# Order of VectorE's work in each step: the lows of a step's weights before the weight sums of the next step

## What is computed

```
f     = relu(einsum('bld,ldf->bf', x, W_enc) + b_enc)   # x: 512 x 2 x 1024, W_enc: 2 x 1024 x 4096
x_hat = einsum('bf,lfd->bld', f, W_dec) + b_dec         # W_dec: 2 x 4096 x 1024
```

## Time and profile before

| | |
|---|---|
| runs | 671.85, 672.27, 672.31 us |
| the profiled execution | 672.02 us |
| its span (first to last instruction) | 670.2 us |
| TensorE busy | 645.5 us, 96% |
| VectorE busy | 577.0 us, 86% |
| ScalarE busy | 339.9 us, 51% |
| mean granted TensorE clock | 0.993 |

### The profile page before, as it was taken

The page is one execution under the profiler, slowest core; times in us unless marked ns, Lnnn a source line. Parts: engine busy times, 40 slices in busy tenths (PEclk is TensorE's granted clock), DMA queues, the critical chain, the costliest instruction groups (busy, mean ns, idle before and its releaser), DMA issues.

```text
span 670.2 us, 8024 instructions
## 1 busy us (share of the span) xinstructions
PE 645.5 (96%) x2892; PEld 525.2 (78%) x2892; DVE 577.0 (86%) x755; ACT 339.9 (51%) x425; POOL 18.3 (3%) x26
## 2 busy tenths in 40 slices
PE   6799999999999999999999999999998999999996
PEld 3577888888887888888888888787876878887785
DVE  6999989889999856659897599999999999997844
ACT  4555335445465445455666657444555454464442
POOL 0000000000000000000000000001102011011000
PEclk9799999999999999999999999999999999999999
DMA  8956676655565565555645475569968889689624
GB/s 299 340 183 195 196 231 187 190 189 179 161 187 184 183 205 172 181 161 173 189 145 189 156 235 191 178 221 225 304 196 230 251 231 270 209 197 308 211 108 156
DMA packets 69446, 137.38 MB, mean 205 GB/s; under 512 B 5152, under 2 KB 5152, under 8 KB 69408
## 3 DMA queue, kind: packets, MB, share of 16 engines
q1 hardware_dynamic: 66528, 126.40, 58.0%
q0 software_dynamic: 2880, 10.49, 8.5%
HBM read 122.18 MB, written 4.19 MB: 189 GB/s over the span
## 4 chain that ended last, share of the span: by engine, by line
PE 69%; DVE 21%; DMA 4%; issue 4%; ACT 1%; SPq 1%; DVEq 0%; ACTq 0%
PE sums L568 22%; PE sums L570 22%; PE sums L569 22%; DVE w_split L368 8%; DVE w_raw L368 5%; PE sums L580 3%; DVE forms L368 3%; DMA w_raw<-w_dec 3%; DVE s_sum L368 2%; DVE place L368 2%; DMA w_raw<-w_enc 1%; ACT w_split L265 0%; ACT place L305 0%; ACT place L318 0%; ACT forms L283 0%
## 5 line engine op out<-in xcount | busy, mean ns | idle before, releaser
L265 ACT CAST w_split<-w_raw 128x1024 fp32r<-128x1024 f32 (+1 forms) x255 | 240.0, 945 | 288.2 <-PE sums L570 225.2
L568 PE MATMUL sums<-w_split,forms 128*128 128x512 f32 x896 | 355.3, 396 | 17.1 <-DVE w_split L368 12.9
L570 PE MATMUL sums<-w_split,forms 128*128 128x512 f32 x896 | 350.1, 391 | 0.0
L569 PE MATMUL sums<-w_split,forms 128*128 128x512 f32 x896 | 349.8, 390 | 0.0
L368 DVE TENSOR_TENSOR w_split<-w_raw,w_split 128x1024 fp32r<-128x1024 f32 (+1 forms) x257 | 269.1, 1082 | 59.6 <-ACT w_split L265 59.0
L568 PEld LDWEIGHTS sums<-w_split,forms 128*128 128x128 f32 x896 | 168.7, 188 | 59.9 <-issue 18.1
L570 PEld LDWEIGHTS sums<-w_split,forms 128*128 128x128 f32 x896 | 168.7, 188 | 36.2
L569 PEld LDWEIGHTS sums<-w_split,forms 128*128 128x128 f32 x896 | 168.9, 189 | 33.6
L368 DVE TENSOR_TENSOR w_raw<-w_raw 128x512 f32<-128x512 f32 x256 | 176.3, 689 | 9.2 <-DMA w_raw<-w_dec 3.7
L368 DVE TENSOR_TENSOR place<-place,sums 128x1024 f32<-128x1024 f32 x26 | 30.5, 1216 | 9.6 <-PE sums L570 7.5
L242 POOL DMA_DIRECT2D place<-place x20 | 17.6, 1008 | 588.0 <-ACT place L305 527.6
(11 more groups left out here) (22 smaller groups left out, 61.9 us busy)
## 6 DMA issues: line engine op xcount, KB each, us to landing
w_raw<-w_dec SPq DMA_DIRECT2D x96, 512.0 KB, 4.9
w_raw<-w_enc SPq DMA_DIRECT2D x94, 512.0 KB, 5.1
place<-place POOLq DMA_DIRECT2D x20, 512.0 KB, 7.8
w_raw<-w_enc SPq DMA_DIRECT2D x36, 256.0 KB, 3.1
w_raw<-w_dec SPq DMA_DIRECT2D x32, 256.0 KB, 3.0
place<-xT SPq DMA_DIRECT2D x8, 512.0 KB, 8.4
outT<-place SPq DMA_DIRECT2D x16, 256.0 KB, 2.2
place<-xT SPq DMA_DIRECT2D x2, 256.0 KB, 3.6
```

What stands on the lines that cost most here:

```text
L265: nc.scalar.copy(split(s, q, 0), w_pos(s, 2 * q, n)).then_inc(hi_done, 1)
L568: nc.tensor.matmul(out, v_hi, w_hi, start=k == 0, stop=False)
L569: nc.tensor.matmul(out, v_lo, w_hi, start=False, stop=False)
L570: last = nc.tensor.matmul(out, v_hi, w_lo, start=False, stop=k == PAIRS - 1)
```

## The change

In VectorE's loop the weight sums of the next step, `w_sums(s + 1)`, go from ahead of both lows of step s to behind them. `lo(s, 1)` keeps its place against the `take_out` calls. Nothing is added or removed, no other engine's list changes, and all waits stay as they are.

```diff
                 for r, i in FORMS_AT.get(s, ()):
                     form_sums(r, i)
-                if s == 0:
-                    lo(s, 1)
-                if s + 1 < STEPS:
-                    w_sums(s + 1)
                 if s:
                     lo(s, 0)
                 if k == 1 and kind in ("dec2", "dec3"):
                     take_out(n - 1, 2)
                 if k == 1 and kind == "enc1":
                     take_out(n - 1, 1)
-                if s:
-                    lo(s, 1)
+                lo(s, 1)
+                if s + 1 < STEPS:
+                    w_sums(s + 1)
                 for r, i in FORMS_AT.get(s, ()):
                     form_lo_direct(r, i)
                     form_lo_sums(r, i)
```

## The result

The changed kernel takes **693.82 us** (four runs, 693.32 to 694.04) against 672.06 for the kernel before (four runs, 671.64 to 672.31). The ratio is 1.032, with a 95% interval of 1.0304 to 1.0335. Forecast were 691.8 us, in a range of 685 to 702. The profiled execution took 694.04 us (span 692.3), 22.0 more than the one of before. Among the runs of the kernel before that the experiments are compared with, one took 1089.83 us at a mean granted clock of 0.557; it is left out of every ratio.

The account below looks back on a forecast made before the run. TensorE was taken as the bound, except at the start and around two chunk borders, where VectorE is late. Terms 9.5 + 2.1 + 7.3 + 0.6 = 19.5 us on the median of 672.27 gave 691.8 us, range 685 to 702.

Parts of the forecast that it names:

- The ring: Four-product steps: VectorE's sums, ScalarE's cast and the lows follow in turn, 5.58 us a round against TensorE's 5.44.
- The start: Steps 0 to 7: VectorE's period stays 6.52 us, but everything TensorE waits for comes 2.06 us earlier.
- Steps 7 to 31: Slow rounds plus take_outs and forms in enc1: step 32 starts at 205.4 instead of 195.9, later by 9.5 us.
- The borders at 40 and 64: Ends of enc2's first and last chunk: a sum gets ahead of four take_outs, 2 x 0.5 us.
- The steps 32 to 79: Forms and take_outs meeting without reserve cost 1 us, two chunk borders 2 x 0.5; together put at 2.1 us.
- Steps 80 to 111: Slow rounds with take_outs and forms: TensorE's stretch takes 187.4 us instead of 180.1, later by 7.3 us.
- Steps 112 to the end: Border at step 120 costs 0.5 us; with the three-product steps after the ring, +0.6 us in all.
- The signs: Expected in the profile: enc1 lows 5.58 us apart, VectorE waiting about 40 us, TensorE idle some 44 us.
- A shorter wait: Rival: VectorE's new wait is nearer 1.05 than 1.25 us, rounds down to 5.38; total 682 us, chance 0.08.
- Copies adding to the ring: Rival: held copies delay TensorE, which delays a cast, 1.75 us more at six borders; 702 us, chance 0.14.
- Faster by an earlier start: Rival: earlier lows gain 2.06 us at the start and up to 3.4 at step 96; 666.8 us, chance 0.02.
- The clock: Rival: eight border waits each set off TensorE's half clock, 2 us a spell; +16, 708 us, chance 0.04.

Follow-up runs that it names:

- e2: Kernel before the change, with ScalarE's first cast waiting only for the first weight sum of its step: 673.48 us, ratio 1.0007.
- e6: Kernel before the change, with the new order only for the sums of steps 80 to 111: 681.65 us, ratio 1.0121.
- e7: Kernel before the change, with the new order only for the single sums of three-product steps: 674.94 us, ratio 1.0028.
- e1: Changed kernel, with ScalarE's first cast waiting only for the first weight sum of its step, not all three: 670.85 us, ratio 0.997.
- e3: Changed kernel, with the next step's weight sums placed between the two lows of a step: 675.69 us, ratio 1.0037 to the kernel before.
- e5: Changed kernel with the first cast's wait shortened and the new order only for four-product steps' sums: 669.68 us, ratio 0.9948 to the kernel before.
- e8: Changed kernel, with ScalarE's third copy_out ahead of the first cast in the step after a chunk's first: 694.11 us, ratio 1.0308 to the kernel before.
- e4: Kernel before the change, with the new order only for the sums of steps 7 to 31: 684.69 us, ratio 1.0177.

## Why the prediction was right, point by point

**The ring.** Forecast 5.58 us from rows in which the same operations stood in another order; the changed kernel shows 5.58 in each plain step. That a low starts 1.14 after the one before, as the rows had it, holds in the ring too: 68.33 to 69.47 for the take_out behind the low in the changed kernel. By the sentence of the Trainium skill that the prediction takes (VectorE: DVE Perf Modes, The DRAIN you can't avoid: the next operation does not start until the pipe empties) the ring would have been 5.75; 5.58 decides for the rows. The same section goes on that a next operation which isn't held starts earlier, so as a whole it leaves room for the rows; the prediction took only its first sentence, where it says that the two differ.

**The start.** VectorE's steps stay at 6.52 and the lows come ahead of the sums, as forecast. In this trace step 6 starts 1.1 earlier, not 2.06: VectorE's first sums of step 1 waited for their load until 14.76, 0.98 later than before (13.78).

```profile
13.78 1.42 DVE L368 TENSOR_TENSOR w_raw<-w_raw 128x512 f32<-128x512 f32 x2 [0.36 <-DMA w_raw<-w_enc]
```

```profile
14.76 2.15 DVE L368 TENSOR_TENSOR w_raw<-w_raw 128x512 f32<-128x512 f32 x3 [0.25 <-DMA w_raw<-w_enc]
```

The first row is of before, the second of the changed kernel. The change doesn't touch what precedes that load. All the traces bear the forecast gain out once it is counted from there: from these sums to TensorE's step 6 it is 40.25 to 40.27 us in the four with the old order in the start (before, e2, e6, e7), and 38.20 or 38.21 in the five with a low ahead of the sums (the changed kernel, e1, e3, e5, e8). That is 2.06 less. The load itself scatters: the sums began between 13.04 and 14.85 in the ten executions. So about 1 us of the 2.5 that the sum was short in the profiled execution belongs to the load. Whether it was late in the other three runs, which took 0.04 to 0.72 us less, no trace shows.

**Steps 7 to 31.** Worked out were 9.5 for step 32 and 1.0 for the steps behind it, with the start's 2.06 in them; with 0.98 for the load that makes 11.5 at step 35, and 11.7 were measured. TensorE's step 32 was forecast at 205.4, which with the 0.98 is 206.4; it began at 206.42.

**The borders at 40 and 64.** 2 x 0.5 forecast, 0.8 and 0.6 measured; e7 has waits of 0.74 and 0.61 there. The steps 32 to 79 together cost 2.4 us (13.0 at step 80 less 10.5 at step 32), 2.1 were forecast, whose two terms add up to 2.0.

**Steps 80 to 111.** This term was the one most too small: 7.3 forecast, 8.1 measured (188.1 us against 180.0). The lows of the steps 80 and 112 began at 420.45 and 608.69, 188.2 apart; the terms of the prediction add up to 188.0, where it writes 187.9. The rest is the reserve at the start of the stretch: step 80 began 1.97 after its low, 1.36 without any reserve, so 0.6 was there and not 1. The third copy's wait in step 80 was foreseen with 1.5 to 1.8 us:

```profile
427.05 0.47 PE L565 MATMUL sums<-w_split,forms 128*128 128x512 f32 x1 [1.74 <-ACT place L305]
```

**Steps 112 to the end.** 0.6 forecast, 1.0 measured: 0.7 from step 112 to step 116, where forms and take_outs meet while there is no reserve, 0.4 at the border of step 120 (a wait of 0.76 against 0.33), and 0.1 won back between them. All four terms were short, by 1.0, 0.3, 0.8 and 0.4; no error hid another.

**The signs.** The casts began after the last sum and the lows came 5.58 apart, as said. Two signs were put too high. VectorE's waits of 1.16 or 1.17 stand ahead of 16 first lows of the steps 7 to 31 and of four of the steps 80 to 111, 23.3 us in all, where about 40 were named. And TensorE is idle for 38.8 us (692.3 - 653.5), not 44: the matmuls last 0.39 us in the profile and start 0.23 apart, so the 0.14 that a step of the ring adds counts as busy. From 93.16 to 98.74 TensorE shows as busy for 5.58 of 5.58 us, with the work of 5.44.

**The rivals.** A shorter wait: refuted by the rows of 5.58. Copies adding to the ring: refuted by e8, where the steps 8 to 31 take the same 141.7 us without that wait. Faster by an earlier start: it needed a cast that begins before the last sum; in the changed kernel that is forbidden, and e1 shows that with just this permitted the sign turns. The clock: see below; one border of the changed kernel had such a spell. Against e8, which had none there, it is 0.6 us more behind at step 97 than at step 96, and nothing more at step 104, since TensorE has to wait for the ring anyway.

## What to carry to other kernels

When two engines hand work to and fro (sums, cast, low), an order is worth what stands *between* the hand-over and the take-back: count the wait that opens when that filling is moved away, add it to the engine's step, and compare with the bound's step before asking what comes earlier. A margin that looks idle (1.11 us a step here) is what pays for irregular work at the borders; once it is gone, every such piece shows up in the total. And look at what the awaiting instruction really reads: here one wait that asked for two sums more than it needed decided over 22 us, while it cost nothing in the old order.

## What was not expected of the hardware

At step 96 TensorE stands for about 2.4 to 2.6 us before a take_out in all of these kernels. In six of the ten profiled executions (the changed kernel, e1, e2, e4, e5, e7) its granted clock fell to half, 1.2 GHz, at the end of that wait or up to 1.3 us behind it, for some 3.4 us; in four (the kernel before, e3, e6, e8) it stayed at 1.00, with waits of the same length. The changed kernel, with the half-clock duration of 0.77 in the first matmul, and e7:

```profile
521.31 0.77 PE L565 MATMUL sums<-w_split,forms 128*128 128x512 f32 x1 [2.44 <-DVE place L368]
```

```profile
506.90 0.80 PE L568 MATMUL sums<-w_split,forms 128*128 128x512 f32 x1 [2.61 <-DVE place L368]
```

The kernel before has its row with 0.50 after 2.63 us of waiting. The prediction had taken that one row as a sign that such a wait is safe; it is safe only sometimes. Seven or eight matmuls start 0.43 instead of 0.23 apart. In e2, e4 and e7 the steps 96 and 97 take 16.1 or 16.2 us with such a spell, in the kernel before 14.5 without one: it costs 1.6 us. Whether this explains why the kernel before scatters from 671.3 to 675.2 us (41 of its 42 runs) was not tested.
